# A quantised MLP stage with its first layer feature-major, and its norm by a total over partitions

## The chip, the cores and the metric

One NeuronCore of a Trainium2 chip runs the whole program. The metric is the device time of one execution in microseconds. The engines are PE (TensorE, matrix products and transposes), DVE (VectorE), ACT (ScalarE), POOL (GpSimd) and SP (SyncE, which issues the DMAs here). Each runs its own list of instructions in order; they meet at semaphores. Their data lies in SBUF, with 128 partitions; PE writes into the 8 banks of PSUM, each 128 x 512 numbers.

## What is computed

An activation `x1` of 8 sequences of 1024 positions and 512 features goes through three layers: a gated delta rule (the first stage), a quantised MLP with low-rank additions (the second stage, which is changed), and a low-rank MLP (the third). The second, cut to what matters:

```python
def _qlora_linear(x, q, scale, bias, la, lb):
    w = _dequant(q, scale)
    base = jnp.einsum('btd,od->bto', x, w) + bias
    lora = jnp.einsum('btr,or->bto', jnp.einsum('btd,rd->btr', x, la), lb)
    return base + lora
h = x
for blk in range(3):
    i0, i1 = (2 * blk, 2 * blk + 1)
    y = _qlora_linear(h, qweights[i0], ...)          # "up"
    y = _layernorm(y, ln_gamma[blk], ln_beta[blk])   # over 512 features, eps 1e-5
    y = jax.nn.gelu(y, approximate=False)
    y = _qlora_linear(y, qweights[i1], ...)          # "down", in the last block "leave"
    h = y + h
```

The weights of all six layers, the low-rank parts added in, are made once, at the end of the first stage. After the second stage the input is added once more and normed over the features; the result is `x3`.

## The kernel before

The second stage (`quantised_and_low_rank_steps`, from line 1185) works in 8 steps of 128 positions. In a step there are two streams `m`, each of 4 sequences, so 512 rows. The three blocks `b` stand inside the step. A unit is one stream and one block of one step: 48 units. Numbers are float32; every product is made of three products of float32r parts, high by high, high by low and low by high, so one 128 x 512 result of one 128-deep chunk is three matmuls (`W_hi`, `W_lo`, `h_hi`, `h_lo`, `g_hi`, `g_lo`).

A unit goes so:
- `enter` (block 0 alone, line 1544): PE turns the input of the stream, 16 transposes, into features by rows in the banks `tr[0..3]`; ACT copies the high part, DVE subtracts for the low part (L1417, L1460).
- `up` (L1555 to L1557): rows by features. The weights of the matmul are a chunk of 128 rows of `h`, the moving operand is `W`. One result bank holds 128 rows with all 512 features, in `lin[0..3]`. ACT writes the bias into the bank ahead (`seed`, L1439). DVE takes mean and variance of each row (bn_stats L1469, aggregate L1471), POOL makes the scale (L1396, L1398), DVE writes the normed row tile to `y[m]` in SBUF (L1484).
- `turn` (L1572): PE turns `y` back, 16 transposes, into `tr`; ACT applies gamma, beta and Gelu twice, once for the high part (L1424) and once in place (L1425), DVE subtracts for the low part (L1491).
- `down` (L1582 to L1584): features by rows, weights stationary; DVE adds bias and residual (L1500, in block 0 L1503 too), ACT and DVE split the new `h`. In the last block it is `leave` (L1601 to L1603): rows by features, with the residual turned in by 4 transposes for each row tile (L1613); DVE adds the input again out of `y[m]`, takes the statistics (L1469, L1471) and scales (L1522) in `y[m]`.
- SP loads `x_in[m]` for the next step when the last `leave` has read it, loads the input again into `y[m]` when the last `turn` has read it, and stores the finished `y[m]` as `x3` (L1357, L1361, L1365).

What sets the order is one list written by hand (`ORDER`), which all engines follow with small changes for PE, DVE and ACT. It interleaves the two streams, so that PE works on one while the other is normed. `leave` of stream 1 falls into the next step's body. The first write of a step into `y[m]` waits for the store of the step before (`x_out`). The first pass through the list runs alone, the other seven in a loop that each engine runs. In the loop of the first stage nothing is changed but the weights' preparation: `tile` on ACT (L720) and `low` on DVE (L886) split each finished weight tile.

Of the kernel before, what the change touches and what calls it, by code (L numbers as in the profile page):

```python
# [15 lines left out]
F32 = mybir.dt.float32  # L16
# [27 lines left out]
def as_f32(ap):  # L44
    return ap.bitcast(F32)
# [42 lines left out]
class KeptInSbuf:  # L88


    def __init__(self, nc, w, shape):
# [8 lines left out]
        self.W_lo = [placed(nc, f"kept_W_lo{l}", tile, F32R, at + layer // 2) for l, at in enumerate(self.W_at)]  # L100
        at = self.small_at = self.base + self.LAYERS * layer
# [16 lines left out]
def delta_rule_and_weights(nc, x, w, consts, masks, x1, q, kept):  # L118
# [22 lines left out]
    with nc.cleanup_on_exit(), ExitStack() as ctx:  # L141
# [13 lines left out]
        def sem(name):  # L155
# [25 lines left out]
         scale, ss, ss_floor, rn, ab, stats, mv, veps, rstd, minus_half, eps, b_qg, minus_mean, shift, nought) = lay(kept.free_at, [  # L181
# [7 lines left out]
            ("minus_half", column, F32), ("eps", column, F32), ("b_qg", [P, 2], F32), ("minus_mean", column, F32), ("shift", column, F32), ("nought", column, F32)], nc.sbuf_usable_end)  # L189
# [60 lines left out]
        def every_second(columns, z):  # L250
# [18 lines left out]
            dequant_done rows_used wT_ps W_hi_done W_lo_done""".split()  # L269
# [330 lines left out]
        def _(act):  # L600
# [125 lines left out]
        def _(dve):  # L726
# [458 lines left out]
def quantised_and_low_rank_steps(nc, x1, w, x3, w_last, out, kept):  # L1185
# [10 lines left out]
    with nc.cleanup_on_exit(), ExitStack() as ctx:  # L1196
# [12 lines left out]
        BIAS_LAYERS = kept.BIAS_LAYERS  # L1209
# [9 lines left out]
        def rows(dram, t, m):  # L1219
# [5 lines left out]
        h_hi, h_lo = zip(*[(sb(f"h_hi{m}", [P, KT, R], F32R), sb(f"h_lo{m}", [P, KT, R], F32R)) for m in range(STREAMS)])  # L1225
        y = per_stream("y", [P, RT, dim])
# [17 lines left out]
        ORDER = []  # L1244

        def put(stage, m, b, parts, behind=0):
            ORDER.extend((stage, m, b, i, behind) for i in parts)

        LAST = BLOCKS - 1
        ROWS, FEATURES = range(RT), range(KT)  # L1250
# [829 lines left out]
```

## Time and profile before

| | |
|---|---|
| median of 3 runs | 2321.88 us (2321.83 to 2322.88) |
| the profiled execution | 2320.67 us, of which span 2318.7 |
| PE busy | 2266.5 us, 98% |
| PE's weight loads (PEld, beside the matmuls) | 1911.4 us, 82% |
| DVE busy | 1537.5 us, 66% |
| ACT busy | 1197.5 us, 52% |
| POOL busy | 786.1 us, 34% |
| mean granted clock of PE | 0.993 |
| first stage / second / third, by PE's first instruction of each | 0 to 607.9 / to about 1832 / to the end |

The profile is of one execution; times in the timelines are microseconds from the start of the span, durations in the groups are the mean of one instruction in nanoseconds. PE's matmuls are pipelined: one shows a duration of 0.39 us but the next starts 0.23 us after it, so pace is read from starts. "Idle before" is how long the engine stood still ahead of an instruction, with what released it.

### The profile page before, as it was taken

The page shows a single profiled execution, that of the slowest core. Times are in us where ns is not written, and L with a number is a line of the kernel's source. Part 1 is how long each engine was busy: PE and PEld are TensorE (multiplying, and loading weights), DVE is VectorE, ACT ScalarE, POOL GpSimd, SP SyncE. Part 2 cuts the span into 40 slices and gives each one's busy share as a digit, 9 for nine tenths or more (in the row PEclk, how much of TensorE's full clock was granted, in tenths as well). Part 3 has the DMA queues.
Part 4 walks back from the last instruction along what each step waited for, and adds up shares of the span by engine and source line. Part 5 has one row for each costly group of instructions (what it writes and reads, how often), then busy time and mean ns, then how long its engine had stood idle before and what let it go on. Part 6 is the DMA issues. An engine that isn't in the chain of part 4 may idle for free.

```text
span 2318.7 us, 37476 instructions
## 1 busy us (share of the span) xinstructions
PE 2266.5 (98%) x12223; PEld 1911.4 (82%) x12223; DVE 1537.5 (66%) x2938; ACT 1197.5 (52%) x2367; POOL 786.1 (34%) x1329
## 2 busy tenths in 40 slices
PE   7999999998899999999999999999999999999997
PEld 6999999997688888888888888888888788888886
DVE  3666666676666666757657666676676766666666
ACT  4455555555534434443443534444344577777775
POOL 2565565566211112112111121111111245555555
PEclk9999999999999999999999999999999999999999
DMA  5122221244201103002021020020211413333322
GB/s 147 56 93 97 100 84 70 100 146 124 93 1 54 56 1 110 0 18 91 0 73 36 18 91 0 18 91 0 89 52 36 164 55 109 109 109 109 109 91 73
DMA packets 101735, 166.38 MB, mean 72 GB/s; under 512 B 19664, under 2 KB 22480, under 8 KB 101520
## 3 DMA queue, kind: packets, MB, share of 16 engines
q1 hardware_dynamic: 97328, 163.69, 20.8%
q10 hardware_dynamic: 4320, 1.71, 0.3%
q8 instruction: 32, 0.52, 0.1%
q14 instruction: 55, 0.45, 0.1%
HBM read 115.05 MB, written 50.33 MB: 71 GB/s over the span
## 4 chain that ended last, share of the span: by engine, by line
PE 71%; DVE 1%; POOL 1%; issue 0%; ACT 0%; POOLq 0%; DVEq 0%
PE quant_bank L1556 7%; PE quant_bank L1555 7%; PE quant_bank L1557 7%; PE quant_bank L1945 6%; PE quant_bank L1947 6%; PE quant_bank L1946 6%; PE quant_bank L1582 5%; PE quant_bank L1583 5%; PE quant_bank L1584 5%; PE quant_bank L1572 4%; PE quant_bank L1601 3%; PE quant_bank L1603 3%; PE quant_bank L1602 3%; PE quant_bank L1544 1%; PE quant_bank L1962 1%; PE quant_bank L1613 1%
## 5 line engine op out<-in xcount | busy, mean ns | idle before, releaser
L1396 POOL TENSOR_SCALAR quant_var<-quant_mv 128x1 f32<-128x1 f32 x256 | 55.6, 217 | 1007.3 <-DVE quant_mv L1471 1007.3
L1424 ACT ACTIVATE quant_g_hi<-quant_bank,kept_beta,kept_gamma 128x512 fp32r<-128x512 f32 x192 | 150.5, 784 | 395.8 <-PE quant_bank L1572 395.8
L1555 PE MATMUL quant_bank<-kept_W_hi,quant_h_hi 128*128 128x512 f32 x768 | 306.0, 398 | 0.0
L1556 PE MATMUL quant_bank<-kept_W_lo,quant_h_hi 128*128 128x512 f32 x768 | 303.9, 396 | 0.0
L1557 PE MATMUL quant_bank<-kept_W_hi,quant_h_lo 128*128 128x512 f32 x768 | 303.6, 395 | 0.0
L1469 DVE BATCH_NORM_STATS2 quant_stats<-quant_bank 128x6 f32<-128x512 f32 x192 | 134.0, 698 | 191.0 <-PE quant_bank L1557 191.0
L1910 DVE TENSOR_TENSOR mlp_g_lo<-quant_bank,mlp_g_hi 128x512 fp32r<-128x512 f32 x256 | 176.4, 689 | 105.1 <-ACT quant_bank L1847 105.0
L1846 ACT ACTIVATE mlp_g_hi<-quant_bank,mlp_b 128x512 fp32r<-128x512 f32 x256 | 177.1, 692 | 71.4 <-PE quant_bank L1947 63.8
L1582 PE MATMUL quant_bank<-quant_g_hi,kept_W_hi 128*128 128x512 f32 x512 | 205.2, 401 | 0.0
L1583 PE MATMUL quant_bank<-quant_g_hi,kept_W_lo 128*128 128x512 f32 x512 | 202.5, 396 | 0.0
L1584 PE MATMUL quant_bank<-quant_g_lo,kept_W_hi 128*128 128x512 f32 x512 | 202.4, 395 | 0.0
L1491 DVE TENSOR_TENSOR quant_g_lo<-quant_bank,quant_g_hi 128x512 fp32r<-128x512 f32 x192 | 130.3, 689 | 99.9 <-ACT quant_bank L1425 97.7
L1439 ACT ACTIVATE quant_bank<-kept_b_all 128x512 f32<-128x512 f32 x192 | 113.3, 603 | 157.3 <-DVE quant_y L1515 85.9
L1557 PEld LDWEIGHTS quant_bank<-kept_W_hi,quant_h_lo 128*128 128x128 f32 x768 | 144.2, 188 | 35.2
L1555 PEld LDWEIGHTS quant_bank<-kept_W_hi,quant_h_hi 128*128 128x128 f32 x768 | 144.3, 188 | 34.3 <-issue 0.2
L1556 PEld LDWEIGHTS quant_bank<-kept_W_lo,quant_h_hi 128*128 128x128 f32 x768 | 144.4, 188 | 34.1
L1847 ACT ACTIVATE quant_bank<-quant_bank,mlp_b 128x512 f32<-128x512 f32 x256 | 168.2, 657 | 0.0
L1484 DVE TENSOR_SCALAR quant_y<-quant_bank,quant_mv,quant_rstd 128x512 f32<-128x512 f32 x192 | 155.5, 810 | 17.2 <-POOL quant_rstd L1398 17.1
L1398 POOL TENSOR_TENSOR quant_rstd<-quant_var,quant_minus_half 128x1 f32<-128x1 f32 x256 | 142.4, 556 | 21.4
L1434 ACT ACTIVATE quant_h_hi<-kept_x_in 128x512 fp32r<-128x512 f32 x128 | 81.9, 640 | 123.8 <-DVE kept_x_in L1503 99.8
L1425 ACT ACTIVATE quant_bank<-quant_bank,kept_beta,kept_gamma 128x512 f32<-128x512 f32 x192 | 145.2, 756 | 0.0
L1805 POOL TENSOR_SCALAR mlp_z<-mlp_z,mlp_mv,mlp_rstd 128x512 f32<-128x512 f32 x60 | 123.8, 2076 | 0.0
(283 smaller groups left out, 5863.2 us busy)
## 6 DMA issues: line engine op xcount, KB each, us to landing
delta_x_in<-L_attn_x_d SPq DMA_DIRECT2D x16, 1024.0 KB, 8.2
delta_x_res<-L_attn_x_d SPq DMA_DIRECT2D x16, 1024.0 KB, 5.5
x_d<-delta_z SPq DMA_DIRECT2D x64, 256.0 KB, 2.1
kept_x_in<-x_d SPq DMA_DIRECT2D x16, 1024.0 KB, 5.2
quant_y<-x_d SPq DMA_DIRECT2D x16, 1024.0 KB, 5.1
x_d<-quant_y SPq DMA_DIRECT2D x16, 1024.0 KB, 5.1
mlp_x_in<-x_d SPq DMA_DIRECT2D x16, 1024.0 KB, 10.3
mlp_x_res<-x_d SPq DMA_DIRECT2D x16, 1024.0 KB, 6.7
```

Source lines behind the costliest of these rows:

```text
L1424: nc.scalar.activation(g_hi[m][:, k, :], tr[k][:, :], ACT.Gelu, bias=beta[:, b, k:k + 1], scale=gamma[:, b, k:k + 1])
L1425: nc.scalar.activation(tr[k][:, :], tr[k][:, :], ACT.Gelu, bias=beta[:, b, k:k + 1], scale=gamma[:, b, k:k + 1]).then_inc(s["gelu_done"], 1)
L1484: nc.vector.tensor_scalar(y[m][:, e, :], lin_of["up", m, b, e][:, :], mv[m][:, e, 0:1], rstd[m][:, e:e + 1], ALU.subtract, ALU.mult).then_ ...
L1555: mm(out, x_hi, W_hi[2 * b][:, k, :], start=False, stop=False, skip_group_check=True)
L1556: mm(out, x_hi, W_lo[2 * b][:, k, :], start=False, stop=False, skip_group_check=True)
L1557: last = mm(out, x_lo, W_hi[2 * b][:, k, :], start=False, stop=k == KT - 1, skip_group_check=True)
L1582: mm(out, W_hi[2 * b + 1][:, k, cols], g_hi[m][:, k, :], start=k == 0, stop=False)
L1583: mm(out, W_lo[2 * b + 1][:, k, cols], g_hi[m][:, k, :], start=False, stop=False)
L1584: last = mm(out, W_hi[2 * b + 1][:, k, cols], g_lo[m][:, k, :], start=False, stop=k == KT - 1)
L1846: nc.scalar.activation(g_hi[:, at, :], p_h[at][:, :], ACT.Gelu_apprx_tanh, bias=b1[:, f:f + 1])
L1847: nc.scalar.activation(p_h[at][:, :], p_h[at][:, :], ACT.Gelu_apprx_tanh, bias=b1[:, f:f + 1]).then_inc(s_["gelu_done"], 1)
L1910: nc.vector.tensor_tensor(g_lo[:, at, :], p_h[at][:, :], as_f32(g_hi[:, at, :]), ALU.subtract).then_inc(s_["g_lo_done"], 1)
```

## The change

The first layer of a block is made feature-major like the second: `W` is stationary, `h` moves, and the result `j` is 128 features by 512 rows in `tr[j]`. The layer norm then goes over partitions and banks:
- The mean is taken out of the weights and the bias. While a tile of an even layer is made, ACT sums it along the output features with an accumulator (times -1/512), and adds that mean to the high part and DVE to the low part. At the start of the second stage ACT does the same with the biases (`b_mid`, `b_root`).
- `square`: ACT writes (result + bias)^2 / 512 of each of the 4 banks to `y[m][:, j, :]`. `part`: POOL adds tiles 1 and 2 to tile 0. `total`: DVE adds tile 3 and eps/128. PE turns the sum, 4 transposes, into the bank `shared`; `spread`: DVE reduces over the 128 partitions' values, POOL takes the power -0.5 of 128 x 4, PE turns that, broadcast to 128 columns, 4 transposes, into `shared` again, ACT copies it to `rstd_row`.
- `normed`: DVE writes (result + bias) x row to `y[m]`; ACT's `gelu` and DVE's `low` read and write `y[m]` in SBUF, and `tr[j]` is free as soon as `normed` has read it.
- `turn`, `seed`, and the row statistics of `up` go. `leave` keeps its own statistics.
- The orders are new and one for each engine. `leave` of both streams now opens the loop's body, with `total` and `spread` of the other stream between its parts, and `up` of block 0 of a stream stands right behind `leave` of the same stream.
- The input of the next step is loaded to `x_next[m]`, in the place of `h_lo[m]`, when the last `up` of the stream is done. `lin` has three banks, the eighth is `shared`.
- The wait for `x_out` stands on ACT's `square` of block 0.

```diff
@@ first stage, ACT and DVE @@
-                nc.scalar.activation(kept.W_hi[l][:, j, :], ring_bank("tile", i)[:, :], ACT.Copy).then_inc(w_["W_hi_done"], 1)
+                if l % 2 == 0:
+                    n = KT * (l // 2) + j
+                    nc.scalar.activation(kept.W_raw[l // 2][:, j, :], ring_bank("tile", i)[:, :], ACT.Copy, scale=-1.0 / dim,
+                                         accum_out=w_mean[:, n:n + 1]).then_inc(w_["w_mean_done"], 1)
+                    act.wait_ge(w_["w_mean_done"], n + 1)
+                    nc.scalar.activation(kept.W_hi[l][:, j, :], ring_bank("tile", i)[:, :], ACT.Identity, bias=w_mean[:, n:n + 1]).then_inc(w_["W_hi_done"], 1)
@@ orders @@
+        def pe_up(m, b):
+            return several("up", m, b, ((0, 0), (1, 0), (0, 1), (1, 1), 2, 3))
+        def pe_between(what, m, b, behind, norm, entering=()):
+            n, a, late = norm
+            return (several(what, m, b, ((0, 0),), behind) + one("total", n, a, late) + several(what, m, b, ((0, 1), (1, 0)), behind) + one("spread", n, a, late)
+                    + several(what, m, b, ((1, 1), 2), behind) + list(entering) + several(what, m, b, (3,), behind))
+        def pe_order():
+            order = pe_between("leave", 0, LAST, 1, (1, LAST, 1), several("enter", 0, 0, KS)) + pe_up(0, 0)
+            order += pe_between("leave", 1, LAST, 1, (0, 0, 0), several("enter", 1, 0, KS)) + pe_up(1, 0)
+            for b in range(LAST):
+                order += pe_between("down", 0, b, 0, (1, b, 0)) + pe_up(0, b + 1)
+                order += pe_between("down", 1, b, 0, (0, b + 1, 0)) + pe_up(1, b + 1)
             return order
+        def act_down(m, b, n, a):
+            order = several("square", n, a, (3,)) + several("high", m, b, (0,)) + one("spread", n, a) + several("high", m, b, (1,)) + several("gelu", n, a, (0, 1))
+            return order + several("high", m, b, (2,)) + several("gelu", n, a, (2,)) + several("high", m, b, (3,)) + several("gelu", n, a, (3,))
+        def dve_leave(m, n, a, late):
+            order = one("total", n, a, late) + one("spread", n, a, late) + several("leave", m, LAST, (0,), 1) + several("normed", n, a, KS, late)
+            order += several("leave", m, LAST, (1,), 1) + several("enter", m, 0, (0, 1, 2)) + several("leave", m, LAST, (2,), 1) + several("enter", m, 0, (3,))
+            return order + several("low", n, a, KS, late) + several("leave", m, LAST, (3,), 1)
+        def dve_down(m, b, n, a):
+            order = one("total", n, a) + one("spread", n, a)
+            for what, i in (("down", 0), ("split", 0), ("normed", 0), ("down", 1), ("normed", 1), ("split", 1), ("normed", 2), ("down", 2), ("normed", 3), ("split", 2),
+                            ("low", 0), ("down", 3), ("low", 1), ("split", 3), ("low", 2), ("low", 3)):
@@ POOL @@
+            def part(t, m, b, j):
+                pool.wait_ge(s["sq_done"], KT * u + j + 1)
+                wait(pool, s["part_done"], 2 * u + j - 1)
+                nc.gpsimd.tensor_tensor(y[m][:, 0, :], y[m][:, 0, :], y[m][:, j, :], ALU.add).then_inc(s["part_done"], 1)
+            def spread(t, m, b, _):
+                pool.wait_ge(s["up_var_done"], u + 1)
+                nc.gpsimd.tensor_tensor(up_rstd[m][:, :], up_var[m][:, :], minus_half[:, :], ALU.pow).then_inc(s["up_rstd_done"], 1)
@@ ACT @@
+            def square(t, m, b, j):
+                act.wait_ge(s["lin_ps"], KT * (BLOCKS * t + b) + j + 1)
+                if b == 0 and j == 0:
+                    wait(act, s["x_out"], 16 * t)
+                nc.scalar.activation(y[m][:, j, :], tr[j][:, :], ACT.Square, bias=b_root[:, b, j:j + 1], scale=ROOT).then_inc(s["sq_done"], 1)
@@ DVE @@
+            def total(t, m, b, _):
+                dve.wait_ge(s["sq_done"], KT * u + KT)
+                dve.wait_ge(s["part_done"], 2 * u + 2)
+                nc.vector.scalar_tensor_tensor(y[m][:, 0, :], y[m][:, KT - 1, :], LN_EPS / P, y[m][:, 0, :], ALU.add, ALU.add).then_inc(s["sum_done"], 1)
+            def spread(t, m, b, _):
+                nc.vector.tensor_reduce(up_var[m][:, :], by_rows, mybir.AxisListType.X, ALU.add).then_inc(s["up_var_done"], 1)
+            def normed(t, m, b, j):
+                nc.vector.scalar_tensor_tensor(y[m][:, j, :], tr[j][:, :], b_mid[:, b, j:j + 1], rstd_row[:, :], ALU.add, ALU.mult).then_inc(s["normed"], 1)
@@ PE @@
+                    mm(tr[j][:, :], W_hi[2 * b][:, k, cols], h_hi[m][:, k, :], start=k == 0, stop=False)
+                    mm(tr[j][:, :], W_lo[2 * b][:, k, cols], h_hi[m][:, k, :], start=False, stop=False)
+                    last = mm(tr[j][:, :], W_hi[2 * b][:, k, cols], h_lo[m][:, k, :], start=False, stop=k == KT - 1)
+            def total(t, m, b, _):
+                pe.wait_ge(s["sum_done"], BLOCKS * t + b + 1)
+                for r in range(RT):
+                    last = nc.tensor.transpose(by_rows[:, r, :], y[m][:, 0, r * P:(r + 1) * P], ident)
+            def spread(t, m, b, _):
+                pe.wait_ge(s["up_rstd_done"], BLOCKS * t + b + 1)
+                for r in range(RT):
+                    last = nc.tensor.transpose(by_rows[:, r, :], up_rstd[m][:, r:r + 1].to_broadcast([P, P]), ident)
```

## Rows read from the trace of the kernel before

**Rows 1.** The stretch view of 608 to 1832 us; the waits of PE.
```profile
608.00:1832.00 1224.00, 1222.58 (x5918) 1003.26 (x5918) 817.92 (x1412) 518.41 (x842) 197.09 (x510) 1.00 0.12 43
...
PE quant_bank L1572 <- DVE quant_y L1484: 1.2, 7, 0.2
```

**Rows 2.** Timeline of SP's queue: residual loads of both streams, consecutive steps (start us, us, engine).
```profile
1022.80 27.91 SPq L1361 DMA_DIRECT2D quant_y<-x_d  x2
...
1174.99 27.91 SPq L1361 DMA_DIRECT2D quant_y<-x_d  x2
```

**Rows 3.** Timeline of PE: matmuls, a group of 16 transposes between them (start us, us).
```profile
1006.02 0.39 PE L1555 MATMUL quant_bank<-kept_W_hi,quant_h_hi 128*128 128x512 f32 x1
...
1017.21 0.40 PE L1582 MATMUL quant_bank<-quant_g_hi,kept_W_hi 128*128 128x512 f32 x1
...
1020.71 1.91 PE L1572 MATMUL quant_bank<-kept_ident,quant_y 128*128 128x128 f32 x16
...
1022.70 0.40 PE L1583 MATMUL quant_bank<-quant_g_hi,kept_W_lo 128*128 128x512 f32 x1
```

**Rows 4.** Groups by line and shape on DVE: count, busy us, mean ns, idle before.
```profile
L1484 DVE TENSOR_SCALAR quant_y<-quant_bank,quant_mv,quant_rstd 128x512 f32<-128x512 f32 x192 | 155.5, 810 | 17.2 <-POOL quant_rstd L1398 17.1
...
L1491 DVE TENSOR_TENSOR quant_g_lo<-quant_bank,quant_g_hi 128x512 fp32r<-128x512 f32 x192 | 130.3, 689 | 99.9 <-ACT quant_bank L1425 97.7
...
L1500 DVE SCALAR_TENSOR_TENSOR kept_x_in<-quant_bank,kept_b_col,quant_h_hi 128x512 f32<-128x512 f32 x64 | 47.7, 746 | 10.6 <-PE quant_bank L1584 10.6
```

**Rows 5.** The same view on ACT.
```profile
L1424 ACT ACTIVATE quant_g_hi<-quant_bank,kept_beta,kept_gamma 128x512 fp32r<-128x512 f32 x192 | 150.5, 784 | 395.8 <-PE quant_bank L1572 395.8
...
L658 ACT ACTIVATE delta_qkT<-delta_p_pj,delta_b_qg 128x512 f32<-128x512 f32 x16 | 11.0, 688 | 8.5 <-PE delta_p_pj L929 8.5
...
L1424 ACT ACT_TABLE_LOAD x1 | 1.3, 1283 | 0.0
```

**Rows 6.** The same view on POOL.
```profile
L1797 POOL TENSOR_TENSOR mlp_x_res<-mlp_x_res,mlp_b_all 128x512 f32<-128x512 f32 x64 | 81.0, 1300 | 10.3 <-DMA mlp_x_res<-x_d 10.3
...
L519 POOL TENSOR_TENSOR delta_rn<-delta_ss_floor,delta_minus_half 128x2 f32<-128x2 f32 x32 | 22.7, 708 | 78.2 <-DVE delta_ss_floor L747 78.2
```

**Rows 7.** Timeline of DVE: stream 1 leaves, with four entering halves between.
```profile
1064.63 0.68 DVE L1515 TENSOR_TENSOR quant_y<-quant_bank,quant_y 128x512 f32<-128x512 f32 x1
...
1066.71 2.48 DVE L1460 TENSOR_TENSOR quant_h_lo<-quant_bank,quant_h_hi 128x512 fp32r<-128x512 f32 x4
1069.11 0.68 DVE L1515 TENSOR_TENSOR quant_y<-quant_bank,quant_y 128x512 f32<-128x512 f32 x1
...
1072.06 0.55 DVE L1522 TENSOR_SCALAR quant_y<-quant_y,quant_mv,quant_rstd 128x512 f32<-128x512 f32 x1 [0.79 <-POOL quant_rstd L1398]
```

**Rows 8.** The store of x3: DMA of 1 MB from issue to landing.
```profile
DMA to landing us min/median/max: 4.1/5.1/6.0
```

**Rows 9.** Timeline of DVE at the end of the loop's body.
```profile
1056.52 0.55 DVE L1522 TENSOR_SCALAR quant_y<-quant_y,quant_mv,quant_rstd 128x512 f32<-128x512 f32 x1 [0.51 <-POOL quant_rstd L1398]
1060.91 0.69 DVE L1515 TENSOR_TENSOR quant_y<-quant_bank,quant_y 128x512 f32<-128x512 f32 x1 [3.85 <-issue]
```

**Rows 10.** PE after two waits, and the granted clock (PEclk) of the stretches that follow.
```profile
607.87 2.67 PE L1544 MATMUL quant_bank<-kept_ident,kept_x_in 128*128 128x128 f32 x16 [2.12 <-PEq L141]
610.19 0.77 PE L1555 MATMUL quant_bank<-kept_W_hi,quant_h_hi 128*128 128x512 f32 x1
...
1836.02 0.50 PE L1945 MATMUL quant_bank<-mlp_g_hi,mlp_U_hi 128*128 128x512 f32 x1 [1.40 <-DVE mlp_g_lo L1910]
...
608.00:613.00 5.00, 5.00 (x24) 4.48 (x24) 2.58 (x4) 4.26 (x8) 0.00 (x0) 0.66 0.00 0
1836.00:1840.00 4.00, 3.98 (x17) 3.22 (x18) 4.00 (x7) 4.00 (x8) 0.00 (x0) 1.00 0.70 262
```

**Rows 11.** Timeline of DVE in the preparation's tail: a low part waits for its high part.
```profile
597.02 0.69 DVE L886 TENSOR_TENSOR kept_W_lo<-delta_p_wide,kept_W_hi 128x512 fp32r<-128x512 f32 x1 [0.41 <-ACT kept_W_hi L720]
```

More of the change, by code:

```diff
@@ L1244, in quantised_and_low_rank_steps @@
-        ORDER = []
-        def put(stage, m, b, parts, behind=0):
-            ORDER.extend((stage, m, b, i, behind) for i in parts)
+        lin = banks[4:7]
+        shared = banks[7]
+        by_rows = shared[:, :].rearrange("p (r n) -> p r n", r=RT)
+        ROOT = 1.0 / math.sqrt(dim)
         LAST = BLOCKS - 1
-        ROWS, FEATURES = range(RT), range(KT)
-        put("leave", 1, LAST, (0, 1, 2), 1)
-        put("enter", 0, 0, FEATURES)
-        put("leave", 1, LAST, (3,), 1)
-        put("up", 0, 0, (0, 1, 2))
@@ L1288, in quantised_and_low_rank_steps, with several @@
-        for m, b, m_down, b_down in TURNS:
-            ORDER_PE.insert(ORDER_PE.index(("turn", m, b, 0, 0)), ("head", m_down, b_down, 2, 0))
-            ORDER_DVE = moved(ORDER_DVE, ("down", m_down, b_down, 2, 0), ("turn", m, b, 1, 0))
-        ORDER_PE.insert(ORDER_PE.index(("turn", 1, LAST, 0, 0)), ("head", 0, LAST, 2, 0))
+        KS = range(KT)
+        FIRST_KS, LAST_K = range(KT - 1), range(KT - 1, KT)
+        def several(what, m, b, parts, behind=0):
+            return [(what, m, b, i, behind) for i in parts]
@@ new lines, in pe_order, with act_leave @@
+        def pe_order():
[4 more added lines that the diff above has]
+                order += pe_between("down", 1, b, 0, (0, b + 1, 0)) + pe_up(1, b + 1)
+            return order
+        def act_leave(m, n, a, late):
+            return (several("square", n, a, (3,), late) + one("spread", n, a, late) + several("gelu", n, a, (0, 1), late) + several("enter", m, 0, KS) + several("gelu", n, a, (2, 3), late))
@@ L1293, in run, with pool_order @@
+        def pool_order():
+            order = one("spread", 1, LAST, 1) + several("leave", 0, LAST, range(RT), 1) + several("part", 0, 0, (1, 2)) + one("spread", 0, 0)
+            order += several("leave", 1, LAST, range(RT), 1) + several("part", 1, 0, (1, 2))
+            for b in range(LAST):
+                order += one("spread", 1, b) + several("part", 0, b + 1, (1, 2)) + one("spread", 0, b + 1) + several("part", 1, b + 1, (1, 2))
+            return order
         def run(eng, stages, order, closing):
@@ L1302, in run @@
                         stages[what](t - behind, m, b, i)
+            for what, m, b, i, behind in order:
+                if behind and what in stages and (what, m) != ("leave", 1):
+                    stages[what](STEPS - 1, m, b, i)
             for word in closing.split():
@@ L1525, in _ @@
             first, steps_of_mlp = mlp["vector"](dve)
-            run(dve, {"enter": enter, "up": up, "turn": turn, "down": down, "leave": leave, **first}, ORDER_DVE,
+            run(dve, {"enter": enter, "total": total, "spread": spread, "normed": normed, "low": low, "down": down, "split": split, "leave": leave, **first}, dve_order(),
                 "leave.0 xT.0 xT.1 U1 leave.1 xT.2 xT.3 leave.2 V1.0 U2.0 P leave.3")
```

312 lines of the change are left out of this document (146 added, 166 removed).

## The prediction

> **What bounds the kernel now.** I read the stretch view first, then PE's waits, then the timelines. From 608 to 1832 us PE is busy 1222.58 of 1224 us at a granted clock of 1.00, and its instructions wait 1.2 us in all [rows 1]. DVE (818), ACT (518) and POOL (197) are half idle or more. So in this stage the number of PE instructions is the time: a step lasts 1174.99 - 1022.80 = 152.19 us [rows 2], 576 products and 160 transposes. 48 products take 1017.21 - 1006.02 = 11.19 us, 0.233 each; 16 transposes push the second product behind them to 1.99 us after their start, so they cost 1.99 - 0.23 = 1.76, 0.11 each [rows 3]. 576 x 0.2333 + 160 x 0.11 = 152.0: the step is explained with nothing left for waits. What the change saves on DVE or ACT is worth nothing by itself; a PE instruction saved is worth its 0.11, and each wait that PE gets is paid in full.
>
> **What PE saves.** Turned rows go: 16 transposes for each of 48 units (8 steps, 2 streams, 3 blocks), 768. The total's columns and the spread row come: 8 for each, 384, of the same shape and so priced alike (they could cost as much as a product, 0.233, if the broadcast operand is slow to load, +47 us; I take 0.11, the row of the nearest kind). The products keep count and shape; the halves of "down" already run with the weights stationary at the same pace. 384 x 0.11 = 42.2 us saved. A step without waits would be 576 x 0.2333 + 112 x 0.11 = 146.7.
>
> **What the other engines do.** DVE loses bn_stats, aggregate and the 0.81 us scaling, and gets in their place one sum, one reduce from PSUM and four multiplications by the row. None of these stands in the trace; the nearest row is scalar_tensor_tensor at 0.746, and tensor_tensor at 0.689 [rows 4], so I take 0.75 for the sum and each multiplication and 0.69 for the reduce (0.5 to 0.9 bounds them). ACT loses the seeds and gets four squares: with a bias operand from PSUM 0.688, each issued some 0.6 after the last [rows 5]. POOL loses four small chains and gets two adds of 128x512, 1.30 each, and one power of 128x4, about 0.7 [rows 6]. Each engine still fits in a step; the question is the order of the chain square, add, add, sum, 4 transposes, reduce, power, 4 transposes, copy, multiply, on which PE now waits twice per unit.
>
> **Where PE waits, by walking the queues with these durations.** I follow each engine's list in its written order.
> First, the plain unit ("down" of one stream, norm of the other). Counted from the end of "up": last square 0.2 to 0.9, sum to 1.75, and PE has 9 products first, to 2.1. Covered, by 0.35 only. The reduce and the power end near 4.3, PE comes for them at 5.35. Covered.
> Second, block 0. DVE has there one more addition for each feature. From the row's copy on it runs multiply, down, add, multiply, split, multiply, down, add, multiply, split, and the third low part ends 7.0 us after the first multiply started, the fourth 10.4. PE comes for the third 0.2 earlier, for the fourth another 0.6 earlier: 0.82 in each of 16 such units, 13.1 us (0 to 25, since the sizes of four unseen instructions decide).
> Third, the loop's end. DVE stands 3.85 us there before its first instruction, although nothing recorded releases it [rows 9]. If ACT does the same (I take it so; 0 is the other end), its last square of stream 1, which is now the first thing in the body, starts some 1.7 late: PE waits 1.05 in each of 7 steps, 7.4 us.
> Fourth, and largest: the squares of block 0 are written into y, and y[m] holds the finished x3 rows of the step before until their store has landed. In the kernel before, half a unit or more lay between; in the new order "up" of block 0 comes directly behind "leave" of the same stream. Zero is the end of the 16 entering transposes. DVE then does three entering halves 1.8, leave row 2 in 2.08 (1064.63 to 1066.71), the fourth half 0.6, four low parts 2.4, and leave row 3 with its power and last scaling 3.5 (1069.11 to 1072.61): 10.4 [rows 7]. The store is issued at once and takes 5.1 (4.1 to 6.0) [rows 8]: 15.5. Two squares 1.3, two adds with their starts 2.9 (POOL starts 0.17 after its releaser), the sum 0.8: 20.6. PE meanwhile: leave row 3 3.2, "up" 11.2, then 4 transposes and 9 products 2.5, or 9 products alone 2.1: it is there at 17.0 or 16.5. It waits 3.6 and 4.1 us. With the small overlaps of the walk 3.66 + 4.10, in 7 steps: 54.3 us. By the ends of the store's landing and an add of 1.26 to 1.6 it is 1.8 to 5.5 each, 25 to 77 us. What ACT has queued behind its waiting square are the next squares only; what DVE has queued behind its sum is the reduce and the next leaving rows, so all of it moves together and nothing is caught up.
>
> **The clock.** PE had 1.0 all through the stage. After the 2.12 us wait at 607.87 the stretch 608 to 613 was granted 0.66, that is partly the 1.2 GHz level, and lost 5 x 0.34 = 1.7 us; after a wait of 1.40 at 1836.02 it stayed at 1.00 [rows 10]. Waits of 3.7 and 4.1 are longer than the one that was followed by a fall, so I charge 1.7 for each of the 14: 23.8 us (0 to 24).
>
> **Once only.** The first step has no leaving rows to fill in: PE waits through the whole first chain and for the entering halves, 1.7 + 1.8 + 2.3 + 1.6 = 7.4. ACT's three sums and four small operations on the biases stand ahead of its first high part: PE's first product, 2.3 us after its first transposes now [rows 10], comes about 2.6 later. The last leaving pass waits 0.7. In the preparation each of 12 weight tiles gets a second pass and an accumulator read on ACT, some 0.85 us; PE and DVE hide most of it while x1 is finished, but at the tail DVE already waits 0.41 for the high part [rows 11]; I take +2 (0 to 10). The x loads now go to h_lo's place after the last "up", over 20 us ahead of their use, against 5 us of landing; SP's new order hides them.
>
> **The sum.** -42.2 + 54.3 + 23.8 + 13.1 + 7.4 + 7.4 + 2.6 + 0.7 + 2 = +69.1. The profiled execution took 2320.67 (2318.7 of span and 2.0 around it), 1.2 below the median of 2321.88. 2320.7 + 69.1 = **2390**.
>
> **Rivals.** (1) The store is hidden: the squares don't wait, because DVE reaches leave row 3 and the landing comes some 4 us sooner than I walk, or PE comes later. Then 54.3 and 23.8 fall away: 2390 - 78 = 2312, and with block 0's waits gone too 2299: faster. It decides where x_out comes 4 us earlier; against it stand the landing's minimum of 4.1 and DVE's steady pace; for it, that PE's margin was read from estimates. (2) A smaller wait that just eats the gain: without store waits the sum is -9.0, so some 0.6 us at each of the 14 visits, without a fall of the clock, gives 2321: no difference. (3) The store waits are there and the clock holds: 2366. (4) Square is not in Gelu's table. The stage now loads its table once, 1.283 us [rows 5]; two more loads per unit would stand ahead of the first square and the first gelu, push the block-0 split and the sums back, and by the walk add some 7.5 us to a step: 2450. The trace shows Square and Sigmoid alternating without a load, but never Square beside Gelu.
> The Trainium skill bears on rival 4: "ScalarE: Activation LUTs", section "Table sets: the hidden batching unit", says that cheap functions are in every set as filler and names relu, copy, identity and abs, not square. The trace agrees for copy and identity, which alternate with Gelu here without a load.
>
> **Chances.** Store waits with the clock's fall 0.58, with the clock held 0.20, table loads 0.06: slower, 0.84. Hidden store: 0.12, faster. Just eaten: 0.04. 0.2% is about what a measurement of this kernel can tell from no change. The range reaches from just below no change, 2318, to 2412, where stores at 6.0 us and adds of 1.5 would lead.
>
> **What would show it.** Of the step: its period in SP's loads, 160 us if right, 149 by rival 1. Of the store: ACT's square of block 0 waiting for a DMA, about 8 to 12 us after its products are there, and PE waiting some 4 us for the DVE sum at both leaving units. Of the clock: PEclk below 1.0 in the stage. Of block 0: PE waiting for h_lo under 1 us. Of the transposes: 8 per unit, 0.11 apart. Wrong would be a stage whose PE stays at 98% busy, or waits at the reduce, the power or the row, which I take as covered.

## The result: 2386.5 us, 2.8% slower, as forecast

The changed kernel takes 2386.52 us (median of 4 runs, 2385.91 to 2388.03), the kernel before 2321.86 beside it (2320.93 to 2322.88). The ratio is 1.028, 95% interval 1.026 to 1.030. The forecast was 2390.0, range 2318 to 2412. The profiled execution of after has a span of 2384.3 us and took 2386.37; before had 2318.7, so 65.6 us more are to be found.

| | before | after |
|---|---|---|
| median, us | 2321.86 | 2386.52 |
| profiled span, us | 2318.7 | 2384.3 |
| PE instructions | 12223 | 11839 |
| first transposes of the stage, us | 607.87 | 618.29 |
| period of a step, us (7 of them) | 152.19 | 158.02 |
| granted clock in the stage | 1.00 | 0.97 |

The stage in the stretch view (us, then busy us and count of PE, PEld, DVE, ACT, POOL, the granted clock, DMA). It answers [rows 1]: where before PE stood still for 1.4 of 1224 us, it now does for 64 of 1292 (6 of these before its first product in the stage, at 622.68), at a granted clock of 0.97. The period forecast was 160 us; it is 158.02.

```profile
608.00:1900.00 1292.00, 1228.14 (x5566) 986.92 (x5566) 715.00 (x1139) 598.05 (x916) 227.95 (x275) 0.97 0.11 41
```

Who is waited for (engine, line, releaser: us in all, times, longest). PE's total waits for DVE's sum, ACT's square for the store (`x_d<-quant_y`). The kernel before has no counterpart to either: nothing in it waited for that store.

```profile
PE quant_bank L1642 <- DVE quant_y L1534: 43.7, 15, 4.4
...
PE quant_bank L1632 <- DVE quant_h_lo L1521: 7.1, 18, 1.1
PE delta_p_wide L1169 <- DVE delta_rows L888: 5.3, 2, 3.5
PE delta_p_tr L1169 <- DVE delta_rows L888: 4.3, 1, 4.3
...
ACT quant_y L1477 <- DMA x_d<-quant_y: 158.7, 14, 12.5
```

SP's queue gives the step (the x loads of stream 0 into their new place): 1204.86 - 1047.69 = 157.17 in this one. The y loads of stream 0 run from 746.62 to 1852.79 in 7 steps, 158.02 each, against 152.19 in [rows 2].

```profile
1047.69 0.40 SPq L1391 DMA_DIRECT2D quant_x_next<-x_d  x1
...
1093.63 31.41 SPq L1399 DMA_DIRECT2D x_d<-quant_y  x2
1204.86 0.40 SPq L1391 DMA_DIRECT2D quant_x_next<-x_d  x1
```

One visit at the sum, put together from the timelines of DVE, SP (just above), ACT, POOL and PE (start us, us). Read it as a chain: DVE's last scaling of x3 ends at 1093.60, the store is issued at 1093.63, the first square starts at 1097.81, 4.2 us later, the adds at 1099.24, the sum at 1101.89, PE's transposes at 1102.63. The square had been ready for 11.16 us.

```profile
1093.05 0.55 DVE L1590 TENSOR_SCALAR quant_y<-quant_y,quant_mv,quant_rstd 128x512 f32<-128x512 f32 x1 [0.78 <-POOL quant_rstd L1449]
...
1097.81 2.42 ACT L1477 ACTIVATE quant_y<-quant_bank,quant_b_root 128x512 f32<-128x512 f32 x4 [11.16 <-DMA x_d<-quant_y]
...
1099.24 2.62 POOL L1431 TENSOR_TENSOR quant_y<-quant_y 128x512 f32<-128x512 f32 x2 [6.29 <-ACT quant_y L1477]
...
1101.89 0.69 DVE L1534 SCALAR_TENSOR_TENSOR quant_y<-quant_y 128x512 f32<-128x512 f32 x1 [8.29 <-POOL quant_y L1431]
...
1099.64 0.40 PE L1685 MATMUL quant_bank<-kept_W_hi,quant_g_lo 128*128 128x512 f32 x1
...
1102.63 1.11 PE L1642 MATMUL quant_bank<-kept_ident,quant_y 128*128 128x128 f32 x4 [2.59 <-DVE quant_y L1534]
1103.40 0.78 PE L1683 MATMUL quant_bank<-kept_W_hi,quant_g_hi 128*128 128x512 f32 x1
1103.97 0.63 PE L1684 MATMUL quant_bank<-kept_W_lo,quant_g_hi 128*128 128x512 f32 x1
1104.40 0.63 PE L1685 MATMUL quant_bank<-kept_W_hi,quant_g_lo 128*128 128x512 f32 x1
...
1106.04 0.39 PE L1684 MATMUL quant_bank<-kept_W_lo,quant_g_hi 128*128 128x512 f32 x1
```

The listed wait is 2.59; by starts it costs 2.99 - 0.23 = 2.76 us, since a product is shown for 0.40 but gives way after 0.233. Behind it the products stand 0.43 apart (1103.97 to 1104.40) and not 0.233, the 1.2 GHz level, until 1106.04: 3.41 us for work that takes 1.80 at full pace (the same sequence behind 1107.91), a loss of 1.61. The other visit of this step costs 3.19 and 1.39.

Experiment 5 has a version with the same list of PE instructions and no slow pace in the steps. Laid beside it, instruction by instruction, the 14 visits to the sum (both streams, 7 steps) cost 44.5 us of waits by starts, and behind every one of the 14 the pace falls for a while, which costs another 24.1 us.

### The profile page after: what moved, and what is told of

Read it like the earlier page. It is cut to its first block, busy times and chain, and to the rows that moved or that the text cites. A ratio compares the mean times of both kernels' runs of the same rounds, so it can differ in the third digit from the quotient of the medians.

```text
span 2384.3 us, 35737 instructions
## 1 busy us (share of the span) xinstructions
PE 2269.7 (95%) x11839; PEld 1894.8 (79%) x11839; DVE 1429.0 (60%) x2650; ACT 1277.5 (54%) x2449; POOL 815.5 (34%) x1089
## 4 chain that ended last, share of the span: by engine, by line
PE 52%; DVE 10%; ACT 5%; DMA 3%; POOL 2%; issue 2%; DVEq 0%; POOLq 0%; ACTq 0%
PE quant_bank L2003 6%; PE quant_bank L2005 6%; PE quant_bank L2004 6%; PE quant_bank L1632 5%; PE quant_bank L1634 4%; PE quant_bank L1633 4%; PE quant_bank L1662 4%; PE quant_bank L1663 4%; PE quant_bank L1664 4%; DMA x_d<-quant_y 3%; DVE quant_g_lo L1552 2%; DVE quant_h_lo L1521 2%; PE quant_bank L1683 2%; PE quant_bank L1684 2%; PE quant_bank L1685 2%
## 5 line engine op out<-in xcount | busy, mean ns | idle before, releaser
L1632 PE MATMUL quant_bank<-quant_h_hi,kept_W_hi 128*128 128x512 f32 x768 | 308.0, 401 | 7.1 <-DVE quant_h_lo L1521 7.1
L1634 PE MATMUL quant_bank<-quant_h_lo,kept_W_hi 128*128 128x512 f32 x768 | 304.2, 396 | 0.0
L1633 PE MATMUL quant_bank<-quant_h_hi,kept_W_lo 128*128 128x512 f32 x768 | 304.2, 396 | 0.0
L1632 PEld LDWEIGHTS quant_bank<-quant_h_hi,kept_W_hi 128*128 128x128 f32 x768 | 144.6, 188 | 55.0 <-DVE quant_h_lo L1521 21.5
L1547 DVE SCALAR_TENSOR_TENSOR quant_y<-quant_bank,quant_b_mid,quant_rstd_row 128x512 f32<-128x512 f32 x192 | 139.1, 745 | 63.1 <-ACT quant_rstd_row L1484 63.1
L1634 PEld LDWEIGHTS quant_bank<-quant_h_lo,kept_W_hi 128*128 128x128 f32 x768 | 144.6, 188 | 35.1
L1633 PEld LDWEIGHTS quant_bank<-quant_h_hi,kept_W_lo 128*128 128x128 f32 x768 | 144.8, 188 | 33.4
L1490 ACT ACTIVATE quant_g_hi<-quant_y,kept_beta,kept_gamma 128x512 fp32r<-128x512 f32 x192 | 155.0, 807 | 12.3 <-DVE quant_y L1547 12.3
L1491 ACT ACTIVATE quant_y<-quant_y,kept_beta,kept_gamma 128x512 f32<-128x512 f32 x192 | 154.5, 805 | 0.0
L1552 DVE TENSOR_TENSOR quant_g_lo<-quant_y,quant_g_hi 128x512 fp32r<-128x512 f32 x192 | 127.6, 685 | 3.8
L1664 PEld LDWEIGHTS quant_bank<-quant_g_lo,kept_W_hi 128*128 128x128 f32 x512 | 98.7, 193 | 24.1
```

What stands on the lines that cost most here:

```text
L1490: nc.scalar.activation(g_hi[m][:, k, :], y[m][:, k, :], ACT.Gelu, bias=beta[:, b, k:k + 1], scale=gamma[:, b, k:k + 1])
L1491: nc.scalar.activation(y[m][:, k, :], y[m][:, k, :], ACT.Gelu, bias=beta[:, b, k:k + 1], scale=gamma[:, b, k:k + 1]).then_inc(s["gelu_done ...
L1552: nc.vector.tensor_tensor(g_lo[m][:, k, :], y[m][:, k, :], as_f32(g_hi[m][:, k, :]), ALU.subtract).then_inc(s["g_lo_done"], 1)
L1632: mm(tr[j][:, :], W_hi[2 * b][:, k, cols], h_hi[m][:, k, :], start=k == 0, stop=False)
L1633: mm(tr[j][:, :], W_lo[2 * b][:, k, cols], h_hi[m][:, k, :], start=False, stop=False)
L1634: last = mm(tr[j][:, :], W_hi[2 * b][:, k, cols], h_lo[m][:, k, :], start=False, stop=k == KT - 1)
```

## The experiments

Each starts from the changed kernel unless it says otherwise. 2386.5 is its time; the kernel before was measured beside every set (2322.2, 2322.1 and 2323.4 us in the three sets).

### 1. The squares in a place of their own

```
-  nc.scalar.activation(y[m][:, j, :], tr[j][:, :], ACT.Square, ...)        # behind a wait for x_out
+  nc.scalar.activation(sq[m][:, j, :], tr[j][:, :], ACT.Square, ...)       # sq[m] lies where g_lo[m] lies
   (the adds, the sum and the total's transposes read sq[m]; the wait for x_out
    stands ahead of DVE's first multiplication by the row, which writes y)
```

> One part of the change undone: the squares of a stream go to a place of their own (where its g_lo lies, free at that time) instead of into y, so ACT no longer waits for the store of x3; that wait now stands ahead of DVE's first multiplication by the row, which comes after the store has landed. Theory (the store holds the squares, PE pays each wait and then a fall of the clock): in the changed kernel the 14 visits cost 2.76 and 3.19 us per step of PE's pace (44.6 us in all by the listed waits of 42.2) and the slow pace behind them 1.6 and 1.4 (20 us); both go, so 2386.5 - 65 = 2322 us, period of a step 148.4, granted clock 1.00 in the stage. Rival (DVE reaches leave row 3 late anyway, or the wait only moves to the multiplication): ACT or DVE waits elsewhere and PE still stalls, 2350 to 2387.

Measured: 2318.41 us, ratio to before 0.998 (0.997 to 0.999). 68 us are gone, as much as the waits and the slow pace cost by PE's starts (44.5 + 24.1 = 68.6). A step lasts 148.23 us (y loads of stream 0 at 1045.24 and 1193.48), the granted clock is 1.00 from 660 to 1800 us, and DVE waits for no store at all: its row's multiplications start at 1085.83, the store was issued at 1075.46. So the wait didn't move, it went. The rival falls.

### 2. The suspected cost doubled

```
   sp.dma_start(rows(x3, t, m), y[m][:, :, :]).then_inc(S[m]["x_out"], 16)
+  sp.wait_ge(S[m]["x_out"], 32 * t + 16)
+  sp.dma_start(rows(x3, t, m), y[m][:, :, :]).then_inc(S[m]["x_out"], 16)   # counts of x_out doubled
```

> The changed kernel with each x3 store done twice, the second time after the first has landed: the suspected cost doubled, nothing else touched. The one store takes 4.2 us from issue to landing, so the squares are held 4.2 to 4.6 us longer at 14 visits: 59 to 64 us, and the two visits that had no fall of the clock get one (3 us): 2446 to 2454 us. If PE's stalls at the sum come from DVE's or POOL's pace and the store's landing only runs beside it, well under half of that: below 2415.

Measured: 2451.09 us, +64.6. The waits' sum grows by 60.0 over 14 visits, 4.3 each, what one store takes.

```profile
PE quant_bank L1644 <- DVE quant_y L1536: 103.7, 15, 8.6
...
ACT quant_y L1479 <- DMA x_d<-quant_y: 218.8, 14, 16.7
```

None of it is absorbed: everything from the store's landing to PE is one chain without slack. The expectation has one premise wrong: there were no visits without a fall that could get one, for all 14 have it in the changed kernel too. The slow pace behind the 14 costs 32.0 us here against 24.1.

### 3. The last piece of the store made small

```
+  for some in (slice(0, RT - 1), slice(RT - 1, RT)):      # rows 0 to 2, then row 3
+      sp.wait_ge(S[m]["x3_done"], RT * t + some.stop)
+      sp.dma_start(rows(x3, t, m)[:, some, :], y[m][:, some, :]).then_inc(S[m]["x_out"], 16)
```

> The changed kernel with the x3 store of each stream and step in two parts: rows 0 to 2 as soon as they are scaled, row 3 alone at the end, so that what lands last is 256 KB and not 1 MB. A dose of the same cause: if the squares wait for the landing (4.2 us now), each of the 14 waits shrinks by what the landing shrinks. Estimated 1.5 to 2.2 us each, 21 to 31 us in all, so 2355 to 2366 us with the clock falling as before, and 2340 to 2350 if the short waits leave the clock alone. If the landing isn't what they wait for, 2386.

Measured: 2364.98 us, in the range, but for another reason than expected. The waits of PE fell by 6.3 us in all (43.7 to 37.4), not by 21 to 31. At the first visit nothing was won, at the second 1.3 us: the last scaling ends at 1091.64 and 1121.47, the squares start at 1096.24 and 1124.36, 4.6 and 2.9 us later.

```profile
1091.09 0.55 DVE L1591 TENSOR_SCALAR quant_y<-quant_y,quant_mv,quant_rstd 128x512 f32<-128x512 f32 x1 [0.79 <-POOL quant_rstd L1450]
...
1120.92 0.55 DVE L1591 TENSOR_SCALAR quant_y<-quant_y,quant_mv,quant_rstd 128x512 f32<-128x512 f32 x1 [0.79 <-POOL quant_rstd L1450]
...
1096.24 2.42 ACT L1478 ACTIVATE quant_y<-quant_bank,quant_b_root 128x512 f32<-128x512 f32 x4 [11.56 <-DMA x_d<-quant_y]
...
1124.36 2.42 ACT L1478 ACTIVATE quant_y<-quant_bank,quant_b_root 128x512 f32<-128x512 f32 x4 [9.73 <-DMA x_d<-quant_y]
```

Row 2 is scaled only 1.3 us before row 3 (the scaling of a row is put off until the next row's statistics are made), so 768 KB go out directly ahead of the 256 KB, and at the first visit the residual's load of 1 MB, issued at 1088.38, is ahead of both. The Trainium skill, "DMA: Bandwidth & Descriptors", section "Queues, rings and completion order", says that a transfer's semaphore increment lands only after every earlier write from that DMA engine. The 4.6 us behind a load and the 2.9 us without one agree with it, but the 4.2 us of a whole store in the changed kernel, with such a load ahead or not, show no difference, and no run here takes the queue apart.

Where do the other 15 of 21.5 us come from? From the clock. Of the 14 visits only 5 are followed by the slow pace, against all 14 in the changed kernel; the six waits of 1.7 us, and three of 2.7 to 3.0, are followed by full pace. One of the six:

```profile
1129.26 0.66 PE L1643 MATMUL quant_bank<-kept_ident,quant_y 128*128 128x128 f32 x4 [1.69 <-DVE quant_y L1535]
1129.68 0.47 PE L1663 MATMUL quant_bank<-quant_g_hi,kept_W_hi 128*128 128x512 f32 x1
```

By PE's starts the slow pace costs 10.6 us here and 24.1 in the changed kernel. These 13.5 and the 6.3 make 19.8 us, against 19.5 by the profiled spans (2384.3 - 2364.8) and 21.5 by the medians.

### 4. The stall filled

```
+  if b == 0 and not (isinstance(t, int) and t == 0):
+      for _ in range(11):
+          mm(shared[:, :], W_hi[2 * LAST + 1][:, 0, 0:P], h_hi[m][:, 0, :], start=True, stop=True)
   pe.wait_ge(s["sum_done"], BLOCKS * t + b + 1)
```

> The changed kernel with 11 products of no use (into the shared bank, 11 x 0.233 = 2.57 us) on PE ahead of the total's transposes of block 0, in the 7 steps in which PE would stand still there for 2.6 us and more. The stall is filled, not shortened. If the falls of the clock come from PE standing still, the slow stretches behind it (1.6 and 1.4 us per step) go: 2386.5 - 20 = 2366 us, granted clock 1.00. If the clock falls for another reason, or the loss behind the stall is not the clock: 2386 to 2388.

Measured: 2363.82 us, 22.7 less, with 154 useless products added. The chain is as long as before (the two visits still cost 2.82 and 3.25 us by starts), only what PE does in it differs. The second visit of a step in PE's timeline:

```profile
1123.70 2.73 PE L1642 MATMUL quant_bank<-quant_h_hi,kept_W_hi 128*128 128x512 f32 x11
1126.95 0.66 PE L1645 MATMUL quant_bank<-kept_ident,quant_y 128*128 128x128 f32 x4 [0.52 <-DVE quant_y L1534]
1127.36 0.48 PE L1665 MATMUL quant_bank<-quant_g_hi,kept_W_hi 128*128 128x512 f32 x1
1127.67 0.39 PE L1666 MATMUL quant_bank<-quant_g_hi,kept_W_lo 128*128 128x512 f32 x1
```

and the stage in the stretch view, the granted clock third from the end:

```profile
660.00:1850.00 1190.00, 1178.16 (x5451) 946.79 (x5450) 676.34 (x1071) 560.23 (x853) 215.38 (x253) 1.00 0.12 42
```

Not one of the 14 visits has the slow pace behind it. So the slow pace comes from PE standing still, and without it the span is 21 us shorter (2384.3 - 2363.4). This is some 3 us less than the 24.1 read from starts: the filled visits are 0.06 us longer each, the stage starts 0.5 us later, and the first step has more slow pace (608 to 660 us were granted 0.77 here, 0.84 in the changed kernel).

### 5. Block 0's order

```
   for what, i in (("down", 0), ("split", 0), ("normed", 0), ("down", 1), ("normed", 1), ("split", 1),
-                  ("normed", 2), ("down", 2), ("normed", 3), ("split", 2), ("low", 0), ("down", 3), ("low", 1), ("split", 3), ("low", 2), ("low", 3)):
+                  ("down", 2), ("normed", 2), ("split", 2), ("down", 3), ("normed", 3), ("split", 3), ("low", 0), ("low", 1), ("low", 2), ("low", 3)):   # where b == 0
```

The term that this tests, in the changed kernel's PE timeline. The third h_lo comes so late that the next product starts 0.40 after the last and the one behind it 0.34, the fourth 0.71 and 0.34; at 0.233 each that is 0.87 us of pace in every one of 16 units, of which only 0.31 are listed as a wait in the unit shown.

```profile
1146.26 0.40 PE L1634 MATMUL quant_bank<-quant_h_lo,kept_W_hi 128*128 128x512 f32 x1
1146.66 0.50 PE L1632 MATMUL quant_bank<-quant_h_hi,kept_W_hi 128*128 128x512 f32 x1
1147.00 0.40 PE L1633 MATMUL quant_bank<-quant_h_hi,kept_W_lo 128*128 128x512 f32 x1
...
1149.33 0.40 PE L1634 MATMUL quant_bank<-quant_h_lo,kept_W_hi 128*128 128x512 f32 x1
1150.04 0.50 PE L1632 MATMUL quant_bank<-quant_h_hi,kept_W_hi 128*128 128x512 f32 x1 [0.31 <-DVE quant_h_lo L1521]
1150.38 0.40 PE L1633 MATMUL quant_bank<-quant_h_hi,kept_W_lo 128*128 128x512 f32 x1
```

> The changed kernel with only DVE's order in the down units of block 0 rewritten: down and split of features 2 and 3 come ahead of multiplications 2 and 3, and the low parts follow at the end. In the changed kernel PE comes too early for the third and fourth h_lo in each of 16 such units, 0.87 us of its pace each (the four gaps in one step: 0.25 + 0.59, twice). Theory: these 13.9 us go and nothing new waits, 2386.5 - 14 = 2372.5 us, and the store's waits stay. Rival: the multiplications come later, so ACT's gelu and the low parts do too, and PE waits at the next down's g_lo or at a bank instead: 2386 or more.

Measured: 2367.64 us, 18.9 less and not 14. The gaps in block 0 are gone and no wait takes their place. The 5 us beyond need not be the edit's: in this execution 11 of the 14 visits have the slow pace behind them, at 18.9 us and not 24.1, and the stage starts at 616.55, 1.7 us earlier. One of the three visits without it comes after 3.67 us by starts, in PE's timeline:

```profile
939.91 0.66 PE L1644 MATMUL quant_bank<-kept_ident,quant_y 128*128 128x128 f32 x4 [3.51 <-DVE quant_y L1536]
940.33 0.48 PE L1685 MATMUL quant_bank<-kept_W_hi,quant_g_hi 128*128 128x512 f32 x1
940.65 0.39 PE L1686 MATMUL quant_bank<-kept_W_lo,quant_g_hi 128*128 128x512 f32 x1
```

The pace stays full for the 14 us behind it.

> Both edits: squares in a place of their own and the new order of block 0. If the two terms are independent and add up: 2318.4 - 14 = 2304.5 us, 0.75% faster than the kernel before, period of a step 146.7 as by 576 products and 112 transposes alone. If the order only helps where the store wait leaves slack, 2318.

Measured, both edits together: 2305.23 us, ratio 0.993 (0.992 to 0.994), 13.2 below the first experiment. From 660 to 1790 us PE has no gap, and a step lasts 1169.67 - 1022.77 = 146.90 us. The first experiment's step lasts 148.23, also at a clock of 1.00, so the clean price of the term is 1.33 us a step, 10.6 in 8 steps; the other 2.6 lie outside the steady steps (the first step is 1.6 us slower there) and in the spread of the first experiment, whose ten runs reach from 2311.56 to 2320.00. The stretch view and SP's timeline:

```profile
660.00:1790.00 1130.00, 1130.00 (x5280) 916.60 (x5279) 684.82 (x1069) 562.50 (x850) 215.35 (x253) 1.00 0.13 44
```

```profile
1022.77 0.40 SPq L1394 DMA_DIRECT2D quant_x_next<-x_d  x1
...
1169.67 0.40 SPq L1394 DMA_DIRECT2D quant_x_next<-x_d  x1
```

### 6. The preparation alone

The kernel before with the centring of the first-layer tiles and nothing else:

```
+  nc.scalar.activation(kept.W_raw[...], ring_bank("tile", i)[:, :], ACT.Copy, scale=-1.0 / dim, accum_out=w_mean[...])
+  nc.scalar.activation(kept.W_hi[l][:, j, :], ring_bank("tile", i)[:, :], ACT.Identity, bias=w_mean[...])
   (DVE's low part adds the same mean)
```

> The kernel before with one part of the change alone: the first-layer weight tiles get the second pass that centres them; the stage itself is the old one (its normalisation takes a mean off anyway). Theory A (the preparation is what starts the stage later): in the changed kernel the stage's first transposes start 10.4 us later than before, so 2321.9 + 10.4 = 2332 us. Theory B (my predicted term): +2, 2324 us, the other 8 us belong to something else of the change.

Measured: 2330.11 us, ratio 1.003 (1.002 to 1.005), 7.9 us slower by the medians, 10.0 by the profiled spans (2328.7 and 2318.7). The stage's first transposes stand at 618.46, in the changed kernel at 618.29, before at 607.87. Theory A holds: the late start comes with the preparation. Not all of the 10.4 us need be its own. Counted back from these transposes, the same PE instruction stands at 178.2 us before and at 179.4 in the changed kernel, and all variants are 0.5 to 1.5 us late there, long before the tiles are made.

The changed kernel shows the road, in the timelines of ACT, DVE and PE. A tile takes ACT two passes and an accumulator read, the tiles stand in a row, ogT_hi stands behind them, and DVE's low parts wait for each tile's second pass and hold back the dequantised rows queued behind them:

```profile
576.64 0.59 ACT L723 ACTIVATE kept_W_raw<-delta_p_tr 128x512 f32<-128x512 f32 x1
577.12 0.20 ACT L723 ACTIVATION_READ_ACCUMULATOR kept_W_raw<-delta_p_tr 128x1 f32 x1
577.35 0.69 ACT L726 ACTIVATE kept_W_hi<-delta_p_tr,delta_w_mean 128x512 fp32r<-128x512 f32 x1
...
576.77 0.75 DVE L896 SCALAR_TENSOR_TENSOR kept_W_lo<-delta_p_tr,delta_w_mean,kept_W_hi 128x512 fp32r<-128x512 f32 x1 [3.24 <-ACT kept_W_hi L726]
...
581.89 0.80 PE L1148 MATMUL delta_p_pj<-delta_wo_hi,delta_ogT_hi 128*128 128x512 f32 x1 [3.35 <-POOL delta_ogT_lo L561]
...
597.95 1.12 PE L1169 MATMUL delta_p_tr<-kept_ident,delta_rows 128*128 128x128 f32 x4 [4.33 <-DVE delta_rows L888]
```

The next version has both edits of experiment 5 and, beside them, two moves in the preparation.

> The same with two moves in the preparation: ACT's ogT_hi ahead of the second passes of one tile (PE stood 3.4 us for what follows from it, before 1.6), and DVE's last scaling of the dequantised rows ahead of the low parts of layer 4, which wait for ACT's two passes. If the 10 us of the preparation are this queueing: the stage starts 3 to 5 us earlier, 2300 to 2302 us. If they are ACT's added time itself, it starts when it did, 2304.

```
-  ... O low.0.2 tile.0.3 lbT.3 low.0.3 ogT dequant.3.1 ...
+  ... O low.0.2 ogT tile.0.3 lbT.3 low.0.3 dequant.3.1 ...
-  tile.4.0 dequant.5.0 low.4.0 tile.4.1 dequant.5.1 low.4.1 tile.4.2 dequant.5.2 low.4.2 tile.4.3 dequant.5.3 low.4.3
+  tile.4.0 dequant.5.0 dequant.5.1 low.4.0 tile.4.1 dequant.5.2 low.4.1 tile.4.2 dequant.5.3 low.4.2 tile.4.3 low.4.3
```

Measured: 2300.85 us, ratio 0.991 (0.990 to 0.992), 4.4 below the version without it. The stage starts at 614.78, 3.9 us earlier than in the version without the moves (618.66) and 3.5 earlier than in the changed kernel. PE's product with ogT_hi starts at 580.87, 1.0 earlier, and now waits for a low part instead; the rest comes from the rows of layer 5. So the order of the queues is worth a third or a little more of the 10 us. The rest was not taken apart. A part of it may be slow pace, for from 540 to 570 us PE was granted 0.89 in the changed kernel against 0.94 before, and from 570 to the stage's start 0.85 against 0.91. This version is the fastest of the study, 21 us (0.9%) below the kernel before.

## Why the prediction was right, term by term

| term | predicted | measured | by |
|---|---|---|---|
| PE's transposes | -42.2 | -42.3 | (146.90 - 152.19) x 8, experiment 5 |
| store waits | +54.3 | +44.6 | 14 listed waits, 42.2, and 0.17 each |
| clock | +23.8 | +24.1 | PE's starts behind the 14 visits; 20.9 by the spans with experiment 4 |
| block 0 | +13.1 | +10.6 | (148.23 - 146.90) x 8, experiment 5; 16 x 0.87 in the gaps is 13.9 |
| loop's end | +7.4 | 0 | no gap there |
| first step | +7.4 | about +9 | listed waits 1.5 + 1.9 + 1.5 + 1.1, and slow stretches |
| bias sums | +2.6 | +2.1 | 622.68 - 618.29 against 2.32 |
| last leave | +0.7 | +0.9 | timeline |
| preparation | +2 | +10.4 | 618.29 - 607.87, experiment 6 |
| way into the last layer | not priced | about +5 | waits of 2.25 and 1.75 us with slow stretches |
| sum | +69.1 | about +64 | found by the spans: 65.6 |

**The transposes.** Right, step and price. In the changed kernel 4 transposes and a product behind them take 0.66 us (1109.05 to 1109.71), so 0.11 each; the row's, with the broadcast operand, take 0.67 (1107.91 to 1108.58), so it costs nothing more.

**The store.** The mechanism is the one forecast, place by place: squares held, both leaving units, PE at the sum. Two sizes were off. Counted from the end of the entering transposes at 1082.9, DVE's last scaling ends 10.7 later (forecast 10.4) and PE comes at 17.0 (forecast 17.0), but the landing takes 4.2 and not 5.1 us. The step of the working that was mis-sized is "takes 5.1 (4.1 to 6.0)" [rows 8], a median from the old order's traffic. The chain is 19.7 long instead of 20.6, 0.9 less at each of 14 visits, 12.6 us; some visits wait longer than the ones read here (4.4 us once), which leaves 9.7.

**The clock.** Right in cause, in number and in size: all 14 visits were charged with 1.7 [rows 10], and all 14 fell, twelve by 1.4 to 1.7 and two by 2.4 and 2.9. The reason given, that a wait longer than one that was followed by a fall will be followed by one too, is weaker than its success. In experiment 5 three visits of 2.75, 2.78 and 3.67 us by starts have full pace behind them, and in experiment 3 three of 2.9 to 3.15 and six of 1.9. So that all 14 fell in the changed kernel didn't follow from the one row, and the exact size is in part luck. Nor does the slow pace always begin at the end of the wait. In this visit of the changed kernel the first products are full (0.23 apart), and from the second group of transposes on they stand 0.43 apart, until 1423.31 (PE's timeline):

```profile
1418.54 0.66 PE L1642 MATMUL quant_bank<-kept_ident,quant_y 128*128 128x128 f32 x4 [2.60 <-DVE quant_y L1534]
1418.95 0.48 PE L1683 MATMUL quant_bank<-kept_W_hi,quant_g_hi 128*128 128x512 f32 x1
...
1420.75 0.63 PE L1684 MATMUL quant_bank<-kept_W_lo,quant_g_hi 128*128 128x512 f32 x1
1421.18 0.63 PE L1685 MATMUL quant_bank<-kept_W_hi,quant_g_lo 128*128 128x512 f32 x1
...
1423.31 0.43 PE L1684 MATMUL quant_bank<-kept_W_lo,quant_g_hi 128*128 128x512 f32 x1
```

**Block 0.** Right: 0.82 a unit forecast, 0.87 found in the gaps and 0.67 by the step's period, from walking DVE's list with durations of neighbours. The unseen instructions came out close: sum 0.69 (taken 0.75), multiplication 0.74 (0.75), reduce 0.69 (0.69), add 1.28 (1.30). Only POOL's power of 128x4 was off, 1.02 and not 0.7, and it lay in covered time. The groups by line on POOL (count, busy us, mean ns, idle before):

```profile
L1431 POOL TENSOR_TENSOR quant_y<-quant_y 128x512 f32<-128x512 f32 x96 | 123.2, 1283 | 649.1 <-ACT quant_y L1477 647.6
L1438 POOL TENSOR_TENSOR quant_up_rstd<-quant_up_var,quant_minus_half 128x4 f32<-128x4 f32 x48 | 49.0, 1020 | 172.9 <-DVE quant_up_var L1540 172.9
```

**The loop's end.** Wrong, and from a misread row. The 3.85 us of [rows 9] look like a gap of an engine that reaches the end of the body with work ready behind it; that is argued, no run tests it. Here ACT and DVE come to the end early and stand there anyway: ACT's first square of the new body starts as PE's product ends, DVE's sum as the last square does. The gap lies inside a wait that was there, and PE pays nothing. The timelines of ACT and DVE there:

```profile
1070.81 0.69 ACT L1477 ACTIVATE quant_y<-quant_bank,quant_b_root 128x512 f32<-128x512 f32 x1 [1.89 <-PE quant_bank L1634]
...
1071.63 0.69 DVE L1534 SCALAR_TENSOR_TENSOR quant_y<-quant_y 128x512 f32<-128x512 f32 x1 [7.47 <-ACT quant_y L1477]
```

**The preparation.** By its own measure the worst term, +2 for +10.4, just outside its own bounds. "PE and DVE hide most of it" was argued from one wait of 0.41 us at the tail [rows 11], not walked. A low part that waits for ACT holds back the rows that PE wants next, so ACT's second pass reaches PE through DVE's queue. Too small by 8, with the unpriced 5 us of the last layer, it offset the loop's end (7 too large) and the landing (10 too large); without that luck the total would not have come out within 4 us.

**The rivals.** The hidden store (rival 1), and with it a wait that just eats the gain (rival 2), was ruled out by the wait for the DMA in the profile and by experiments 1 and 2. Its price is telling all the same: 2312 was forecast for the kernel without store waits, and the version built for it takes 2318, 6 more: the preparation's 8 and the last layer's 5 on one side, the loop's end's 7 on the other. The clock that holds (rival 3, 2366) was ruled out by the granted clock of 0.97 and by the slow pace behind the visits; experiment 4, which brings that about, took 2363.82. Table loads (rival 4) didn't come: ACT has the same four loads as before, 1.283 us each, one of them at the first gelu of the stage (L1490), with squares and gelus alternating behind it.

## What to carry to other kernels

Before giving a buffer a second use as scratch, ask what still reads it and when that reader is done: here the squares took the place of finished rows on their way to memory, and against 42 us of saved PE time stood 69 us of waits and slow pace; another place for the same squares, with no more memory, gave 68 us back. Where one engine sets the time, walk every queue that feeds it in written order with durations of neighbours, also in the stretches that look like a detail, for a short wait in front of a queue is paid by what is queued behind it. Price a stall of TensorE as its length and, apart from that, as what the granted clock takes afterwards, and test the second by filling the stall. To see whether the pace fell, read on for some microseconds behind the wait and not only the first products.

## What the runs showed of the hardware

- Behind all 14 waits of the changed kernel (2.8 to 4.6 us by starts) the pace fell to half, in most for 3 to 4 us, in two for longer, and at some it fell only about 1 us after work had begun again. Behind waits of the same lengths it fell in 11 of 14 cases in experiment 5 and in 5 of 8 in experiment 3. Of six waits of 1.9 us by starts (1.7 listed) in experiment 3 none was followed by it, of 14 waits of 6.8 to 8.6 us listed in experiment 2 all were.
- A store of 256 KB behind 768 KB of the same rows landed 2.9 us after its data was ready, behind 768 KB and a load of 1 MB 4.6. 1 MB in one transfer takes 4.2 in the changed kernel, at the visit with such a load 3.3 us ahead of it and at the one without. So the small last piece won 1.3 us at one visit and nothing at the other; what it wins with nothing ahead of it was not run.
- POOL's power takes 0.54 us for 128x1 (L1449) and 1.02 for 128x4.
- DVE's scaling of dequantised rows takes 0.68 us at most places, 1.70 at 596.20 and 1.76 at 598.71; why was not looked into.
